# A 32-wide state product of a linear-attention block, laid into eight small tiles of the TensorE array

## What is computed

```
Q, K, V = xn @ W_Q, xn @ W_K, xn @ W_V   per head; Q and K get rotary angles and position scales
scores  = (Q @ K.T) * gamma_h**(n - m)   for m <= n, else 0
Y       = scores @ V                     per head, then normalised per head, times gn_weight, plus gn_bias
attn    = (silu(xn @ W_G) * Yn) @ W_O
```

## Time and profile before

| | |
|---|---|
| median of 3 runs | 910.05 us (909.77 to 910.67) |
| the profiled execution | 908.67 us, of which the span from first to last instruction is 906.9 us |
| TensorE clock granted | 0.994 of full |
| PE busy | 870.9 us (96%) |
| VectorE (DVE) busy | 834.6 us (92%) |
| GpSimd (POOL) busy | 673.4 us (74%) |
| ScalarE (ACT) busy | 493.7 us (54%) |

### The profile page before, as it was taken

How to read it: one execution, slowest core, us unless ns; L and a number is a source line. 1 busy time by engine, 2 the same in 40 slices (tenths; PEclk the granted TensorE clock), 3 DMA queues, 4 the chain that set the end, 5 groups by cost and what they waited for, 6 DMA issues and landing times.

```text
span 906.9 us, 20369 instructions
## 1 busy us (share of the span) xinstructions
PE 870.9 (96%) x7698; PEld 762.5 (84%) x7698; DVE 834.6 (92%) x1883; ACT 493.7 (54%) x1358; POOL 673.4 (74%) x791
## 2 busy tenths in 40 slices
PE   1879999999999999999999999999999999999996
PEld 1668888888888888888888888888888888888885
DVE  7879999999999999999999999999999999999984
ACT  4555555555555555555555555555555555555552
POOL 5467777777778777777877777787777778777773
PEclk9999999999999999999999999999999999999998
DMA  9200110110111011011101101110110110110000
GB/s 339 69 1 19 36 37 18 37 37 19 36 36 36 19 37 35 19 36 36 31 24 36 37 18 37 35 32 23 36 33 22 37 37 26 29 37 12 8 13 18
DMA packets 30049, 33.62 MB, mean 37 GB/s; under 512 B 3328, under 2 KB 28672, under 8 KB 29696
## 3 DMA queue, kind: packets, MB, share of 16 engines
q1 hardware_dynamic: 29808, 32.26, 11.3%
q10 hardware_dynamic: 144, 0.07, 0.0%
HBM read 23.92 MB, written 8.39 MB: 36 GB/s over the span
## 4 chain that ended last, share of the span: by engine, by line
PE 94%; DVE 2%; POOL 1%; ACT 1%; DMA 1%; issue 0%; SPq 0%; POOLq 0%
PE quad L882 12%; PE quad L880 12%; PE quad L881 12%; PE quad L1057 5%; PE quad L941 4%; PE quad L964 4%; PE bank L880 3%; PE bank L881 3%; PE bank L882 3%; PE bank L996 3%; PE quad L1064 3%; PE quad L908 3%; PE quad L1041 2%; PE quad L965 2%; PE quad L929 2%; PE quad L933 2%
## 5 line engine op out<-in xcount | busy, mean ns | idle before, releaser
L880 PE MATMUL quad<-w_gu_hi,xqT_hi 128*128 128x512 f32 (+1 forms) x384 | 149.9, 390 | 3.0 <-DVE xqT_lo L586 3.0
L882 PE MATMUL quad<-w_gu_hi,xqT_lo 128*128 128x512 f32 (+1 forms) x384 | 145.2, 378 | 0.0
L881 PE MATMUL quad<-w_gu_lo,xqT_hi 128*128 128x512 f32 (+1 forms) x384 | 144.4, 376 | 0.0
L461 POOL TENSOR_TENSOR rstd<-var_eps,power 128x9 f32<-128x9 f32 x67 | 124.6, 1860 | 5.6
L452 POOL TENSOR_TENSOR x_quot<-xn,x_inv 128x256 f32<-128x256 f32 x64 | 41.0, 640 | 90.3 <-DVE x_inv L630 90.2
L469 POOL TENSOR_TENSOR xT_lo<-xT_in,xT_hi 128x256 fp32r<-128x256 f32 x64 | 47.0, 734 | 64.8 <-ACT xT_hi L775 64.8
L438 POOL TENSOR_TENSOR h_quot<-h,h_inv 128x704 f32<-128x704 f32 x64 | 88.9, 1389 | 6.3 <-DVE h_inv L577 1.3
L714 ACT ACTIVATE xqT_hi<-bank 128x256 fp32r<-128x256 f32 x64 | 24.5, 383 | 120.6 <-PE bank L916 120.6
L448 POOL TENSOR_TENSOR qk<-qk_cos,qk_sin 128x512 f32<-128x512 f32 x64 | 82.9, 1296 | 9.1 <-DVE qk_cos L589 1.4
L485 POOL TENSOR_TENSOR gate_gn<-gate,gn 128x512 f32<-128x512 f32 x64 | 82.7, 1292 | 0.2 <-ACT gate L768 0.2
L880 PEld LDWEIGHTS quad<-w_gu_hi,xqT_hi 128*128 128x128 f32 x384 | 72.6, 189 | 11.7 <-issue 3.2
(11 more groups left out here) (176 smaller groups left out, 2943.4 us busy)
## 6 DMA issues: line engine op xcount, KB each, us to landing
x_in<-in_x_dram SPq DMA_DIRECT2D x64, 128.0 KB, 2.2
xT_in<-in_xT_dram SPq DMA_DIRECT2D x64, 128.0 KB, 2.2
out_dram<-y_out SPq DMA_DIRECT2D x64, 128.0 KB, 1.7
sin<-const_sin_dram SPq DMA_DIRECT2D x1, 1792.0 KB, 10.9
raw<-in_w_gu_dram SPq DMA_DIRECT2D x2, 512.0 KB, 6.6
w_qkvg<-in_w_qkvg_dram SPq DMA_DIRECT2D x1, 1024.0 KB, 7.2
cos<-const_cos_dram SPq DMA_DIRECT2D x1, 896.0 KB, 7.0
raw<-in_w_down_dram SPq DMA_DIRECT2D x2, 352.0 KB, 7.3
```

The lines of the kernel that those rows point to most:

```text
L461: pool.tensor_tensor(rstd[:, (t + 3) % RING, :], var_eps[:], power[:], ALU.pow).then_inc(rstd_ready, 1)
L880: pe.matmul(out, hi[:, k], w_hi[:, k], start=start, stop=False)
L881: pe.matmul(out, hi[:, k], w_lo[:, k], start=False, stop=False)
L882: return pe.matmul(out, lo[:, k], w_hi[:, k], start=False, stop=stop)
```

## The change

- The state's product is made of eight matmuls of 32x32 array tiles, one for each head, straight from the summed state (128x64). It stands directly ahead of the values' product, behind the turns of xq, z and the hidden layer. Its waits on `state_copy` and `masked1` are gone.
- For the second group of heads, head r's queries and keys lie one quarter of the partitions further on (`ORDER`, `place`), so that its tile is at rows of quarter r+1 and columns of quarter r; the first group's tiles are on the diagonal. The values are not moved.
- ACT's four copies, the tile `state_sum` and the clearing of `state` are gone; DVE adds into `state` (128x64).
- The ring `rstd` has 16 numbers per slot instead of nine, of which nine are used.

```diff
+ORDER = [*range(HG), *(HG + (r - 1) % HG for r in range(HG))]
...
-        rstd = sb("rstd", [P, RING, 1 + H])
+        rstd = sb("rstd", [P, RING, 16])
...
-        state_sum = sb("state_sum", [P, G * HD])
-        state = sb("state", [P, D])
+        state = sb("state", [P, G * HD])
...
+        def quarter(r):
+            return slice(r * HD, (r + 1) * HD)
+        def place(g, r):
+            return quarter((r + g) % HG)
...
-            pool.memset(state[:], 0.0).then_inc(cleared, 1)
...
-                        dve.tensor_tensor(state_sum[:], state_sum[:], b_kv[:, 0:G * HD], ALU.add).then_inc(kv_add, 1)
+                        dve.tensor_tensor(state[:], state[:], b_kv[:, 0:G * HD], ALU.add).then_inc(kv_add, 1)
...
-                    act.wait_ge(kv_add, kept_upto(t))
-                    for r in range(HG):
-                        rows = slice(r * HD, (r + 1) * HD)
-                        ins = act.activation(tiles(state[:])[rows, :, rows], heads(state_sum[:])[rows], ACT.Copy)
-                    ins.then_inc(state_copy, 1)
...
-                if exists(i - 1) and later(i - 1):
-                    t = i - 1
-                    pe.wait_ge(state_copy, kept_upto(t - 1))
-                    pe.wait_ge(masked1, t + 1)
-                    for g in range(G):
-                        ins = pe.matmul(b_yT[g], state[:, g * P:(g + 1) * P], qT[:, g, :], start=True, stop=False)
-                    ins.then_inc(st_ready, 1)
...
                     ins.then_inc(h1_turned, 1)
+                if exists(i - 1) and later(i - 1):
+                    t = i - 1
+                    for g in range(G):
+                        for r in range(HG):
+                            rows = place(g, r)
+                            ins = pe.matmul(b_yT[g][quarter(r), :], state[rows, g * HD:(g + 1) * HD], qT[rows, g, :], start=True, stop=False)
+                    ins.then_inc(st_ready, 1)
...
-                            ins = pe.matmul(b_yT[g][rows, :], val[:, head:head + HD], probs[:, r, g * P:(g + 1) * P],
+                            ins = pe.matmul(b_yT[g][quarter(r), :], val[:, head:head + HD], probs[:, (r + g) % HG, g * P:(g + 1) * P],
...
-                            ins = pe.matmul(b_kv[rows, g * HD:(g + 1) * HD], qk[:, D + head:D + head + HD], val[:, head:head + HD],
+                            ins = pe.matmul(b_kv[place(g, r), g * HD:(g + 1) * HD], qk[:, key:key + HD], val[:, head:head + HD],
...
+    w_q, w_k = w_q[ORDER], w_k[ORDER]
```

More of the change, by code:

```diff
@@ L53, in tables @@
     for way in (1, -1):
-        for h in range(H):
+        for h in ORDER:
             size = scale ** (way * pos / SCALE_BASE) * np.exp(way * pos * log_gam[h])
@@ L283, in block_kernel @@
         x_high = sem("x_high")
-        state_copy = sem("state_copy")
         x_normed = sem("x_normed")
         qk_ready = sem("qk_ready")
-        st_ready = sem("st_ready")
         x_turned = sem("x_turned")
@@ L293, in block_kernel @@
         h1_turned = sem("h1_turned")
+        st_ready = sem("st_ready")
         yT_ready = sem("yT_ready")
@@ L424, in _ @@
             pool.memset(moments[:], 1.0).then_inc(cleared, 1)
-            pool.memset(state[:], 0.0).then_inc(cleared, 1)
-            pool.wait_ge(cleared, 3)
+            pool.wait_ge(cleared, 2)
             def step(i):
@@ L460, in step @@
                     pool.wait_ge(var_ready, t + 4)
-                    pool.tensor_tensor(rstd[:, (t + 3) % RING, :], var_eps[:], power[:], ALU.pow).then_inc(rstd_ready, 1)
+                    pool.tensor_tensor(rstd[:, (t + 3) % RING, 0:1 + H], var_eps[:], power[:], ALU.pow).then_inc(rstd_ready, 1)
                 if exists(i - 1):
@@ L464, in step @@
                     pool.wait_ge(rstd_ready, t + 4)
-                    pool.tensor_tensor(heads(y_gain[:]), heads(gate_gn[:, t % 2, 0, :]), spread(rstd[:, (t + 3) % RING, 1:], HD), ALU.mult).then_inc(gain_ready, 1)
+                    pool.tensor_tensor(heads(y_gain[:]), heads(gate_gn[:, t % 2, 0, :]), spread(rstd[:, (t + 3) % RING, 1:1 + H], HD), ALU.mult).then_inc(gain_ready, 1)
                 if exists(i + 1):
@@ L609, in step @@
                     if t == 0:
-                        dve.wait_ge(cleared, 3)
+                        dve.wait_ge(cleared, 2)
                     dve.wait_ge(x_stats, t + 1)
@@ L659, in step @@
                     if t % CHUNKS == 0:
-                        dve.tensor_copy(state_sum[:], b_kv[:, 0:G * HD]).then_inc(kv_add, 1)
+                        dve.tensor_copy(state[:], b_kv[:, 0:G * HD]).then_inc(kv_add, 1)
                     else:
-                        dve.tensor_tensor(state_sum[:], state_sum[:], b_kv[:, 0:G * HD], ALU.add).then_inc(kv_add, 1)
+                        dve.tensor_tensor(state[:], state[:], b_kv[:, 0:G * HD], ALU.add).then_inc(kv_add, 1)
                 if exists(i):
@@ L775, in step @@
                     act.activation(xT_hi[:], xT_in[:, t % SLOTS], ACT.Copy).then_inc(x_high, 1)
-                if exists(i - 1) and kept(i - 1):
-                    t = i - 1
-                    if t == 0:
-                        act.wait_ge(cleared, 3)
-                    act.wait_ge(kv_add, kept_upto(t))
-                    for r in range(HG):
-                        rows = slice(r * HD, (r + 1) * HD)
-                        ins = act.activation(tiles(state[:])[rows, :, rows], heads(state_sum[:])[rows], ACT.Copy)
-                    ins.then_inc(state_copy, 1)
                 if exists(i + 2):
@@ L855, in load_functions @@
             def load_functions():
-                act.wait_ge(cleared, 3)
+                act.wait_ge(cleared, 2)
                 act.activation(scratch[:], power[:], ACT.Silu)
@@ L902, in step @@
                         turn_rest(8)
-                if exists(i - 1) and later(i - 1):
-                    t = i - 1
-                    pe.wait_ge(state_copy, kept_upto(t - 1))
-                    pe.wait_ge(masked1, t + 1)
-                    for g in range(G):
-                        ins = pe.matmul(b_yT[g], state[:, g * P:(g + 1) * P], qT[:, g, :], start=True, stop=False)
-                    ins.then_inc(st_ready, 1)
-                if exists(i):
-                    t = i
                     if t == 0:
@@ L939, in step @@
                         for r in range(HG):
-                            rows, head = slice(r * HD, (r + 1) * HD), (g * HG + r) * HD
-                            ins = pe.matmul(b_yT[g][rows, :], val[:, head:head + HD], probs[:, r, g * P:(g + 1) * P],
+                            head = (g * HG + r) * HD
+                            ins = pe.matmul(b_yT[g][quarter(r), :], val[:, head:head + HD], probs[:, (r + g) % HG, g * P:(g + 1) * P],
                                             start=t % CHUNKS == 0, stop=True)
@@ L949, in step @@
                         for r in range(HG):
-                            rows, head = slice(r * HD, (r + 1) * HD), (g * HG + r) * HD
-                            ins = pe.matmul(b_kv[rows, g * HD:(g + 1) * HD], qk[:, D + head:D + head + HD], val[:, head:head + HD],
+                            key, head = D + g * P + place(g, r).start, (g * HG + r) * HD
+                            ins = pe.matmul(b_kv[place(g, r), g * HD:(g + 1) * HD], qk[:, key:key + HD], val[:, head:head + HD],
                                             start=True, stop=True)
```

## The result

The changed kernel takes 907.94 us (median of 20 runs, 906.98 to 909.09) against 909.93 us of the kernel before on the same occasions (20 runs). The ratio is 0.9978, interval 0.9971 to 0.9984: 2.0 us faster, with 1.5 to 2.6 us as its bounds. The forecast was 912.0 us, 2 us slower.

What follows compares the result with a forecast made beforehand. PE was taken as the bound, its step paid out in full. Per step 0.382 - 0.340 = +0.04 us, +2.4 us in all, or +1.7 by another count; the mean, +2 us, moved 910.05 to 912.0 us, range 903.0 to 919.0.

Steps and rivals of the forecast that it cites:

- Taking L908 away: On PE, dropping the old state's product (four instructions) saves 0.34 us per step, -19.0 us over 56 steps.
- The wait for z: Without L908, PE asks for z before POOL ends it; a wait of 0.09 us returns in every step.
- Adding the eight tiles: On PE, the new state's product ahead of the values' product (L941) costs 0.382 us a step, +21.4 us.
- Two rounds: The 16 instructions on eight 32x32 tiles run eight at once, in two rounds of 0.108 us.
- the stagger of 0.007: Tiles of a round start 0.007 us apart; seven places add 0.047 us to the new state's product.
- the empty 0.09 us: PE does nothing for 0.092 us at the new boundary from 32x32 to 128x32 tiles, ahead of L941.
- Four rounds with the gap: Upper bound for the new state's product if the two groups of tiles take turns: 0.573 us a step.
- The other edits: ACT's copies, DVE's add, dropped waits, clearing, rotated order, wider ring: about 0; for moved tiles, 1 us either way.
- No gap: Rival: no empty time between 32x32 and 128x32 tiles; -0.12 us per step, 903 to 904 us; chance 0.18.
- the eight tiles don't run together: Rival: the rotation buys nothing, four rounds; +0.23 us per step, +13 us, 923 us; chance 0.22.
- smaller gains: Chance 0.07 beside the no-gap rival: a gap half as long (about 909 us) or z earlier (up to 5 us).

Runs made afterwards that it cites:

- one shape: Kernel before with the state's product moved directly ahead of the values' product, as eight matmuls of 128 rows and 32 columns, the values' product's tile shape: 915.60 us, ratio 1.0063.

## Why the prediction was wrong

- **"Taking L908 away", -0.340 us a step: right.** The wait for z came back in every step, at the size of the first-chunk steps.
- **"Adding the eight tiles", 0.382 us: right.** 0.378 was measured. Two rounds, the stagger of 0.007 and the empty 0.09 us at the new change of shape are all there; the rounds have a run of their own (without the turn), and so has the gap (one shape).
- **The sum of these, +0.04 us a step and +2 us: right for what it covers.** With the ring undone the kernel is at 1.0021 of the kernel before, +1.9 us, and the forecast was 912.0 against 910.05. (Four rounds with the gap add up to 0.571 in the prediction, not 0.573; nothing hangs on it.)
- **"The other edits": this is the step that failed.** It took the moved tiles at 0 "and leave 1 us either way". Alone they are worth -0.53% (0.40 to 0.65), 4.2 us by the medians, and in the changed kernel they turn +0.2% into -0.2%. The comparison behind it was of L1137 with L908: matmuls of 128 columns, and by their recorded lengths, which don't tell what a matmul costs PE. The effect is mainly in the matmuls of 512 and 384 columns; those of 256 lose a little. There are 24 of 512 columns in a step, and they take about 24 x 0.233 = 5.6 us, so 1 us over 64 steps claimed that their pace would hold to 0.3%, on a row of another shape. With the ring alone the 24 went from 5.670 to 5.595 us, 1.3% less, and the six of the value-and-gate product by 2.9%. That the power's duration doesn't depend on its ring slot was true and beside the point: the ring mattered by its size alone, which puts `xT_hi` at 128 modulo 256. Nothing in the profile of before gave the price or its sign, but it did give the room. Its value-and-gate matmuls followed one another at 231 to 235 ns, and the fastest of 512 columns at 229. At 229 for all 24, and without the weight load that is exposed once a step, a step would be 0.09 us shorter, some 6 us in all (an estimate from these starts). Bounds of that size around the forecast would have reached below the time of the kernel before.
- **The rivals.** "No gap" and "the eight tiles don't run together" both fell. The measured time lies inside the range of 903.0 to 919.0 us and near the "smaller gains" of the forecast, but those stood for half a gap or an earlier z, and neither happened. That the range holds it is luck.

Left open: why the value-and-gate product is fast with the x tiles at 128 modulo 256 while the query-key product hardly gains, and what the down product answers to. With all places equal, the part of the down product behind the value-and-gate product takes 1.296 us in the usual steps of the kernel before and 1.311 in its first-chunk steps, so something besides the places has a share too. It may be what other engines read and write at that moment; no run separates this.

## What to carry to other kernels

An edit of a tile's size moves every tile behind it; where one engine is the bound and reads wide operands, such a move is an edit of its own, to be run alone, and its bounds should be at least the room between the pace of those matmuls and the best pace in the trace (here 6 us, and 4 came). Steps of a pipeline that leave out a piece of work (a first chunk) price that piece, its hidden waits included, far better than its own rows do. A list of waits that goes by recorded lengths can miss a wait of 0.1 us in every step. And a gain in a stretch that another engine's chain spans is not paid out until the instruction that waits for that chain stands later.

## What the runs showed of the hardware that was not expected

- In the value-and-gate product, a matmul of 512 columns with fp32r operands went at 226.7 or 233.3 ns from start to start, by where the x tiles (its stationary tile among them) start modulo 256 bytes: 128 is fast (up to 228.1 with other tiles elsewhere), 0, 160 and 192 are slow. The query-key product, from the same stationary tiles, went only from 232.6 to 231.4. A move by 256 changed no product by more than 1 ns, and moves by 96 and by 352 gave the same step to 0.3 ns (13.2877 and 13.2879 us).
- Eight 32x32 tiles take 16 passes in two rounds, starts 7 ns apart, also where two tiles share rows or columns. Two matmuls on one tile don't overlap (0.569 us instead of 0.378 for eight on four tiles).
- A change from 32x32 to 128x32 tiles costs the same 0.09 us of nothing as the changes that involve full-array shapes; between 128x32 and 128x32 there is none.
